# A two-layer convolution kernel: ScalarE takes the fourth quarter's exponential and the third quarter's eviction one slot earlier

## The reference

```python
x = x + _L0_conv_ref(_gn(x), g_pos, g_neg, bias, input_factor, output_factor)
x = x + _L1_conv_ref(_gn(x), Wq, Wk, Wv, B, Wm)
```

```python
q, k, v = Wq @ xf, Wk @ xf, Wv @ xf
ek = jnp.exp(k); eB = jnp.exp(B)
out = Wm @ (q * ((eB @ (ek * v)) / (eB @ ek)))
```

## Time and profile before

| what | us |
|---|---|
| median of 3 runs | 1547.64 |
| lowest and highest | 1546.84, 1547.73 |
| the profiled execution | 1546.89 |
| its span, from first to last instruction | 1545.1 |
| TensorE, VectorE, ScalarE, GpSimd busy | 1446.8, 1403.4, 1189.6, 521.5 |

### The profile page before, as it was taken

The page is one execution under the profiler, slowest core; times in us unless marked ns, Lnnn a source line. Parts: engine busy times, 40 slices in busy tenths (PEclk is TensorE's granted clock), DMA queues, the critical chain, the costliest instruction groups (busy, mean ns, idle before and its releaser), DMA issues.

```text
span 1545.1 us, 24432 instructions
## 1 busy us (share of the span) xinstructions
PE 1446.8 (94%) x8560; PEld 645.9 (42%) x8560; DVE 1403.4 (91%) x2185; ACT 1189.6 (77%) x1561; POOL 521.5 (34%) x503
## 2 busy tenths in 40 slices
PE   2799999999999999999999999999999999999975
PEld 1444444444444444444444444444444444444432
DVE  6879999999999999999999998999999999998866
ACT  4557788788878878887887888788787978876563
POOL 3111334333433433333343333334333333433312
PEclk9799999999999999999999999999999999999998
DMA  5011012223122222312222231221323122112222
GB/s 206 1 55 42 14 28 56 82 55 110 42 63 88 56 82 56 110 42 63 88 56 83 55 110 39 59 96 42 96 55 109 33 65 96 42 41 56 63 75 82
DMA packets 29180, 103.91 MB, mean 67 GB/s; under 512 B 4032, under 2 KB 4224, under 8 KB 29056
## 3 DMA queue, kind: packets, MB, share of 16 engines
q1 hardware_dynamic: 20416, 70.86, 12.3%
q0 software_dynamic: 8640, 31.46, 10.8%
HBM read 37.29 MB, written 33.55 MB: 46 GB/s over the span
## 4 chain that ended last, share of the span: by engine, by line
DVE 52%; PE 27%; issue 12%; ACT 7%; POOL 1%; DMA 1%; DVEq 1%; SPq 0%; ACTq 0%; POOLq 0%
DVE xr L1228 5%; PE A L504 5%; PE A L505 5%; PE A L506 5%; DVE duo L1132 3%; DVE uall L1225 3%; DVE A L1195 3%; DVE A L1204 3%; DVE uall L1198 3%; DVE duo L1192 3%; DVE uall L1200 2%; DVE duo L1193 2%; DVE A L1196 2%; DVE f L1109 2%; PE B L504 2%
## 5 line engine op out<-in xcount | busy, mean ns | idle before, releaser
L504 PE MATMUL A<-T,WH 128*128 128x504 f16 (+1 forms) x1152 | 438.4, 381 | 0.0
L506 PE MATMUL A<-T,WL 128*128 128x504 f16 (+1 forms) x1152 | 437.3, 380 | 0.0
L505 PE MATMUL A<-T,WH 128*128 128x504 f16 (+1 forms) x1152 | 437.3, 380 | 0.0
L1521 POOL TENSOR_TENSOR T<-t,T 128x512 f16<-128x512 f32 x189 | 254.6, 1373 | 442.4 <-ACT T L766 442.4
L1495 POOL TENSOR_TENSOR zl<-z,zh 128x512 f16<-128x512 f32 x120 | 159.5, 1346 | 434.5 <-ACT zh L877 434.5
L809 ACT ACTIVATE junk<-xr,shift 128x1024 f16<-128x1024 f32 x244 | 280.2, 1148 | 29.6 <-DVE xr L1228 24.2
L504 PE MATMUL B<-T,WH 128*128 128x504 f16 (+1 forms) x576 | 221.7, 385 | 20.0 <-DVE T L1158 11.5
L505 PE MATMUL B<-T,WH 128*128 128x504 f16 (+1 forms) x576 | 221.8, 385 | 0.0
L506 PE MATMUL B<-T,WL 128*128 128x504 f16 (+1 forms) x576 | 221.5, 384 | 0.0
L504 PEld LDWEIGHTS A<-T,WH 128*128 128x128 f16 x1152 | 115.4, 100 | 164.2 <-issue 46.3
L506 PEld LDWEIGHTS A<-T,WL 128*128 128x128 f16 x1152 | 112.7, 98 | 136.2
(11 more groups left out here) (186 smaller groups left out, 2564.7 us busy)
## 6 DMA issues: line engine op xcount, KB each, us to landing
xr<-in_x_dram SPq DMA_DIRECT2D x64, 512.0 KB, 5.7
out_dram<-xr SPq DMA_DIRECT2D x64, 512.0 KB, 2.7
xr<-shared POOLq DMA_DIRECT2D x60, 512.0 KB, 4.5
xr<-in_L_conv_g_pos_dram SPq DMA_DIRECT2D x3, 576.0 KB, 9.3
xr<-in_L_conv_g_neg_dram SPq DMA_DIRECT2D x3, 576.0 KB, 10.5
xr<-in_L_conv_Wm_dram SPq DMA_DIRECT2D x2, 32.0 KB, 9.0
xr<-in_L_conv_Wq_dram SPq DMA_DIRECT2D x1, 32.0 KB, 11.4
xr<-in_L_conv_Wk_dram SPq DMA_DIRECT2D x1, 32.0 KB, 11.2
```

The lines of the kernel that those rows point to most:

```text
L504: nc.tensor.matmul(to, wh, th, start=fresh and y == 1, stop=False, skip_group_check=True)
L505: nc.tensor.matmul(to, wh, tl, start=False, stop=False, skip_group_check=True)
L506: done = nc.tensor.matmul(to, wl, th, start=False, stop=y == 2, skip_group_check=True)
L1521: last = nc.gpsimd.tensor_tensor(low, t32[:, pair, :, :, :].rearrange("p t e w -> p (t e w)"), high, ALU.subtract)
```

## The change

Two numbers of ScalarE's tables go from 45 to 44:

```diff
-KV_ACT = (21, 32, 39, 45)
-MIX_ACT = (32, 40, 45, 57)
+KV_ACT = (21, 32, 39, 44)
+MIX_ACT = (32, 40, 44, 57)
```

## The result

| what | before | changed |
|---|---|---|
| median, us | 1547.24 (4 runs) | 1532.05 (4 runs) |
| lowest and highest, us | 1546.43, 1547.73 | 1531.66, 1532.22 |
| the profiled execution, us | 1546.89 | 1532.11 |
| its span, us | 1545.1 | 1530.4 |

The ratio is 0.991, with a 95% interval of 0.9898 to 0.9922: the changed kernel is about 0.9% faster. A second comparison on another occasion gave 1531.9 (4 runs) against 1546.53 (7 runs), ratio 0.9903, 0.9887 to 0.992. The forecast was 1534.0, in a range of 1531 to 1541.

A forecast was written before the change was run, and what follows sets the result against it. The prediction took a ScalarE queue order, felt in a cycle through VectorE and TensorE, as the bound. 12.7 us for phases 2 to 14 plus 0.85 made 13.6 us: 1533.3 for the profiled execution, 1534.0 forecast as median, range 1531 to 1541.

The forecast's parts named there:

- What bounds the kernel: ScalarE delays exponential and eviction behind statistics; a VectorE-TensorE cycle sets the 90.22 us period, TensorE having about 0.5 us room.
- The exponential and L1280: ScalarE's exponential moves ahead of the statistics, so VectorE's L1280 starts right behind L1088, 0.90 to 0.98 us earlier.
- The queries: In slot 10 TensorE's weight-load gap before the queries falls from 1.45 to 0.43 us, a gain of 1.02 us.
- The statistics and `guess`: ScalarE's quarter 2 statistics follow the eviction, leaving 0.3 to 0.4 us idle before `guess`; VectorE's L1076 keeps 2.6 us room.
- The shared port: GpSimd's L1521 slows VectorE in slots 8 and 9, but its distance to L1228 stays, leaving 0.90 to 0.98 us.
- Rival B: GpSimd's L1521 stretches VectorE's earlier L1280, perhaps L1192, swallowing the gain: 1544.2 or 1547.6 us; chance 5%.
- its end may be what sets the earliest start of L1280: The end of GpSimd's L1521 at 877.95, just as L1088 ends at 877.98, may limit how early VectorE's L1280 starts.
- that the trace bears the full blocking out only in part: L1228 and L1521 run side by side for 3.30 us, L1228 lengthened by 0.95 us, so full blocking seemed only partly supported.
- The sum: 13 x 0.98 = 12.7 us in phases 2 to 14 plus 0.85 us in phase 15, together 13.6 us.
- A: Another semaphore keeps TensorE's gap at the queries above 0.43 us, halving the gain to 7.1 us: 1540.5; chance 18%.
- C: Slower: a late mix holds up ScalarE's queue past VectorE's slot 12, one us beyond costing 14 us: 1561.6; chance 4%.
- D: The period falls by TensorE's full 1.02 us and part of its 0.53: 18 us, 1529.6; chance 3%.

The follow-up runs named there:

- the third experiment: The changed kernel with VectorE's channel sums of the next image moved from slot 9 to slot 10: 1526.78 us, ratio 0.9874 to the kernel before.
- The second pair: Both kernels measured and traced once more without further edits, changed kernel against the kernel before: 1531.9 us against 1546.53.

## Why the prediction was right, point by point

- *What bounds the kernel* (a queue order on ScalarE, one cycle over VectorE and TensorE with 0.5 us of room for TensorE): confirmed from four sides. By the period, VectorE's release alone is worth 0.48 us (the room), TensorE's alone is worth nothing and costs 2.06 us through the exponential, both together 0.99, and VectorE's further 0.65 us again only 0.53.
- *The exponential and L1280*: forecast 0.98 us, with 0.90 as a lower bound. Measured lead per phase: 2.70 - 1.72 = 0.98 at the first. The choice of 0.98 by the overlap of L1088 and L1288 was the right one.
- *The queries*: forecast a gap of 0.43 us and a gain of 1.02; the gap is 0.43.
- *The statistics and `guess`*: forecast 0.3 to 0.4 us of idle in front of `guess`; 0.34 measured. What the prediction said of the cover behind it was incomplete. It named only L1076, 2.6 us later. The first to feel a late `guess` is TensorE, through `copy_queries`, and with no cover to speak of: a slip of `guess` by 0.5 us arrived as 0.49 us. It was harmless for another reason, TensorE's room later in the phase.
- *The shared port*: the page cited there, the Trainium skill's "SBUF — State Buffer", "Who interferes with whom", exempts a VectorE instruction with at most one SBUF input outside the two-port modes. The trace of the third experiment agrees: L1280 and L1192 keep 0.69 and 0.68 us beside L1521, while L1088 there had needed 0.97. L1088 reads no PSUM; whether it falls under the two-port modes is not shown here. Rival B falls with that, by measurement. The step "its end may be what sets the earliest start of L1280" was true of the order as it stood, since L1088 in front of L1280 ends with L1521 in each trace, but L1280 itself was never held. One reading of the prediction was wrong here, without effect on its sum: that the trace bears the full blocking out only in part. The row merges three instructions. One by one, in the kernel before, they are:

```profile
872.52 1.15 POOL L1521 TENSOR_TENSOR T<-t,T 128x512 f16<-128x512 f32 x1 [0.30 <-ACT T L766]
...
873.63 3.20 POOL L1521 TENSOR_TENSOR T<-t,T 128x512 f16<-128x512 f32 x1
...
876.79 1.15 POOL L1521 TENSOR_TENSOR T<-t,T 128x512 f16<-128x512 f32 x1
```

  L1228 starts with the first and is 0.95 us longer than in slot 23. The second lasts 3.20 us instead of 1.15 and ends 1.02 us after L1228. L1088 ends at 877.98, 0.04 us after the third. This looks like engines that take turns by whole instructions, so the trace fits the blocking that the prediction quotes. No experiment here isolates it.
- *The sum*: 13 x 0.98 + 0.85 = 13.6 us. The second pair has 12.90 + 1.00 = 13.9, the first 13.21 + 0.94 less the 1.1 us of the tail, 13.1. The medians showed 14.6 and 15.2 us. The rest, 0.7 us in the second pair and 2.1 in the first, is not the change's as far as the traces tell: 1.72 us of the first profiled pair was there before the first changed instruction ran. That it is chance and no effect of the program rests on two traces of each kernel (154.48 and 155.50; 152.76 and 155.10), and on the clock between 80 and 90 us, which sorts all seven. The traces show only one execution each, so how much of a median is such chance is not shown. The measured 1532.05 us lies at the low edge of the forecast's own 1532 to 1537; the mechanism was right, and the number stayed inside the range with 1 us to spare.
- *Rivals*: A (TensorE's gap only half closed) did not occur, B is refuted, C (ScalarE's queue as a new bound) did not occur, and a further copy of 1.04 us on that queue cost next to nothing, D (more than VectorE's own gain) is excluded by the period of 89.23.

The period in the loop fell by 0.99, a little over 0.98. The one of the thirteen in which the loop turns fell by 1.27 us in the first pair and by 0.73 in the second; the exponential alone gave 1.42 us there in its trace. That one stays unexplained.

## What to carry to other kernels

Where two engines hand over to each other in one cycle, find for each of them how much it could gain alone; the time follows the smaller, and a wait that has become short tells how much room the other side has. Moving one entry of a pair is not half of the gain: here it was half, or a loss of twice the gain. And an edit has to be judged on the kernel on which it will stand: the same move of five small instructions was worth about -5 us with this change and +10 us without it.

## What the runs showed that was not expected

- Programs that issue the same instructions up to that point reach the residual of phase 1 up to 3.7 us apart (152.27 to 155.94 us), and the granted clock between 80 and 90 us, 0.83 to 1.00, tells the late from the early. For a change worth 13 us that is a quarter of it, so the distance between two marks inside the steady part (12.90 and 13.21 us) is a sharper measure than the medians.
- Five small instructions on VectorE take 2.24 us from first start to last end in slot 9 beside GpSimd, and 0.99 us in slots 10 and 12, with L1082 and L1088 lengthened to 0.74 and 0.97 us, while instructions of 512 columns that read PSUM beside the same GpSimd instruction keep their 0.69 us.
